# Chunk 0 of a Mamba-style block: its x-projection moved into its convolution, copies a block later, late weight halves on GpSimd

## Reference

```python
x = x + 0.5 * ffn(layernorm(x))      # gate and up 512 -> 1408, silu(g) * u, down -> 512
x = x + mamba(layernorm(x))
x = x + 0.5 * ffn(layernorm(x))
```

```python
proj = einsum('blh,oh->bol', x, W_in); h, gate = split(proj, 2)    # 1024 channels each
h = silu(causal_conv4(h) + conv_b)
ts, B, C = split(einsum('bil,oi->blo', h, Wx), [128, 144])         # the x-projection: 128 + 16 + 16
ts, B, C = rms(ts), rms(B), rms(C)
delta = softplus(Wdt.T @ ts + dt_bias)
s_t = exp(delta_t * A) * s_(t-1) + delta_t * B_t * h_t             # 16 states a channel
y = (sum_n s_t * C_t + D * h) * silu(gate)
return y @ Wout.T
```

## Time and profile before

| | us |
|---|---|
| median of 3 runs | 2893.6 (2881.7 to 2895.21) |
| the profiled execution | 2891.33 |
| its span, first to last instruction | 2889.4 |
| DVE busy in it | 2494.8 |
| PE busy in it | 2412.0 |
| POOL busy in it | 2261.2 |
| first scan starts at | 203.0 |

### The profile page before, as it was taken

One profiled execution on the slowest core, in us unless ns is written; L12 is line 12 of the kernel. 1 busy time (PEld: TensorE's weight loads), 2 busy tenths in 40 slices (PEclk: granted clock), 3 DMA queues, 4 the chain that ended last, 5 costly groups with the idle time before them and its releaser, 6 DMA issues. The chain is left out here.

```text
span 2889.4 us, 38162 instructions
## 1 busy us (share of the span) xinstructions
PE 2412.0 (83%) x12266; PEld 1949.8 (67%) x12266; DVE 2494.8 (86%) x3131; ACT 1757.7 (61%) x2995; POOL 2261.2 (78%) x1371
## 2 busy tenths in 40 slices
PE   6668879788787998889988899889988896599968
PEld 5556667567566776677766777667766775377757
DVE  5559999799888999899989989798988988999973
ACT  5456568667466666576657666667656667465532
POOL 2237859988977989689996889779896899889852
PEclk9789889899888999899998999889999997599979
DMA  7644563674686367955777376964678478355544
GB/s 266 224 149 161 183 228 114 227 258 128 226 286 238 120 203 254 326 163 185 233 262 275 124 221 224 315 211 148 222 256 287 132 263 300 111 192 189 189 163 142
DMA packets 293951, 606.65 MB, mean 210 GB/s; under 512 B 23024, under 2 KB 23792, under 8 KB 293744
## 3 DMA queue, kind: packets, MB, share of 16 engines
q1 hardware_dynamic: 293744, 604.13, 62.4%
HBM read 451.47 MB, written 152.57 MB: 209 GB/s over the span
## 5 line engine op out<-in xcount | busy, mean ns | idle before, releaser
L1893 POOL TENSOR_TENSOR sbuf<-dus,bring 128x1024 f32<-128x1024 f32 x512 | 1222.0, 2403 | 236.2 <-PE pt L1369 128.5
L1520 ACT ACTIVATE pa<-dls,cst 128x512 f32<-128x512 f32 x1024 | 691.4, 688 | 424.2 <-DVE sbuf L1694 416.7
L1369 PE MATMUL pt<-ident,sbuf 128*128 128x128 f32 x4096 | 662.8, 299 | 227.1 <-DVE sbuf L1694 100.6
L1369 PEld LDWEIGHTS pt<-ident,sbuf 128*128 128x128 f32 x4096 | 517.1, 153 | 392.9 <-DVE sbuf L1694 142.3
L1288 PE MATMUL pm<-xT,wring 128*128 128x512 f32 x2816 | 707.8, 400 | 12.7 <-ACT pm L1420 5.5
L1694 DVE TENSOR_TENSOR_SCAN sbuf<-pa,sbuf 128x512 f32<-128x512 f32 x512 | 607.7, 1209 | 61.6 <-ACT pa L1520 52.9
L1694 DVE TENSOR_TENSOR_SCAN sbuf<-pa,carry,sbuf 128x512 f32<-128x512 f32 x512 | 634.5, 1266 | 26.4 <-ACT pa L1520 18.7
L1705 DVE SCALAR_TENSOR_TENSOR acc<-pt,cT,acc 128x512 f32<-128x512 f32 x768 | 547.5, 737 | 76.2 <-PE pt L1369 72.4
L1300 PE MATMUL pm<-wring,act 128*128 128x512 f32 x2176 | 577.8, 408 | 30.4 <-DVE hd L1622 10.3
L1288 PEld LDWEIGHTS pm<-xT,wring 128*128 128x128 f32 x2816 | 518.5, 190 | 115.8 <-issue 15.3
L1311 PE MATMUL pm<-xT,wring 128*128 128x512 f32 x1536 | 430.5, 432 | 79.5 <-DVE hd L1644 27.4
(11 more groups left out here) (130 smaller groups left out, 2266.6 us busy)
## 6 DMA issues: line engine op xcount, KB each, us to landing
wring<-wsp SPq DMA_DIRECT2D x408, 512.0 KB, 4.5
bring<-b_d SPq DMA_DIRECT2D x256, 256.0 KB, 3.9
xn_d<-tb SPq DMA_DIRECT2D x24, 1024.0 KB, 9.8
xnb<-xn_d SPq DMA_DIRECT2D x19, 1024.0 KB, 7.9
x_d<-tb SPq DMA_DIRECT2D x16, 1024.0 KB, 6.2
u_d<-hd SPq DMA_DIRECT2D x64, 256.0 KB, 4.9
sg_d<-hd SPq DMA_DIRECT2D x64, 256.0 KB, 4.4
tb<-x_d SPq DMA_DIRECT2D x16, 1024.0 KB, 7.1
```

What stands on the lines that cost most here:

```text
L1369: ins = e.matmul(pt[u.pt[tt]][:, k * P:(k + 1) * P], sbuf[:, u.s3, k, tt * P:(tt + 1) * P], ident[:, :], is_transpose=True, start=True, st ...
L1520: e.activation(pa[k % 2][:, :], dls[:, k, :], ACT.Exp, scale=col(C_A + (4 * u.ig + k) * N + u.n)).then_inc(S.a_exp, 1)
L1893: e.tensor_tensor(sbuf[:, u.s3, h * m:(h + 1) * m, :], dus[:, h * m:(h + 1) * m, :], bring[:, u.s2:u.s2 + 1, :].broadcast_to([P, m, TC]), ...
```

## The change

Four things change. First, in chunk 0 the steps of the x-projection are listed inside the convolution: step 0 behind block 6's projection, step 1 behind block 7's, steps 2 to 6 behind the last block. They add to the two banks of `pt`, blocks 4 and 5 are made in the two banks of `pa` (six banks for the projection), and there is a fourth tap row. Second, ACT's copy and POOL's subtraction of block i are listed behind the end of block i + 1, in every chunk (`conv_lift`). Third, the last step and `x_out` of chunk 0 are a stage `x_end`, and three of the eight gates stand between it and `dt0`. Fourth, the low halves of the 16 late pieces are made by POOL and no longer by DVE.

```diff
+AHEAD0 = 6
+GATES0 = 3
-OPENING = (("ffn1", 0), ("prep_in", 0), ("dt0", 0), ("gates", 0), ("dt2", 0), ("dt3", 0), ("ffn1", 1),
+OPENING = (("ffn1", 0), ("prep_in", 0), ("x_end", 0), ("gates_a", 0), ("dt0", 0), ("gates_b", 0), ("dt2", 0), ("dt3", 0), ("ffn1", 1),
...
-        u.lo = self.up(self.S.v_piece)
+        u.lo = self.up(self.S.g_piece if late else self.S.v_piece)
...
-        keys = ("aa", 0), ("aa", 1), ("th", 0)
+        keys = ("aa", 0), ("aa", 1), ("th", 0), ("th", 1)
+        x_banks = [(NM + 2, (self.flag,)), (NM + 3, ())]
...
-            u.h, u.key = i % (2 if c else 3), i % 3
+            u.h, u.key = i % (2 if c else 3), i % (3 if c else 4)
...
-            u.bank, u.bank_before = self.bank()
+            if c == 0 and i in (NM, NM + 1):
+                u.bank, u.bank_before = i, ()
+            else:
+                u.bank, u.bank_before = self.bank()
...
+            elif not c and i >= AHEAD0:
+                self.x_step(c, i - AHEAD0, x_banks)
             self.nested(i)
         while opened:
             self.conv_end(opened.pop(0), keys)
+        if self.lifts:
+            self.conv_lift(self.lifts.pop())
...
+        if c == 0:
+            for k in range(NI - AHEAD0, NI - 1):
+                self.x_step(c, k, x_banks)
+            for k in range(2):
+                self.sfree["pa", k] = self.bank_free[NM + k]
+            self.to_close = c, x_banks
+            return
...
         self.free[keys[v.key]] = self.bank_free[v.bank] = (v.u,)
-        v.hi = self.up(S.a_chi)
-        v.lo = self.up(S.g_clo)
+        if self.lifts:
+            self.conv_lift(self.lifts.pop())
+        self.lifts.append(v)
+
+    def conv_lift(self, v):
+
+        S = self.S
+        w = self.add("c", self.step_of(v, "conv_lift"))
+        w.hi = self.up(S.a_chi)
+        w.lo = self.up(S.g_clo)
...
+        if c == 0:
+            for h in range(2):
+                self.sfree["pt", h] = (u.sq[h],)
...
+        elif kind == "x_end":
+            self.close_x()
+        elif kind == "gates_a":
+            self.gates(c, range(GATES0))
+        elif kind == "gates_b":
+            self.gates(c, range(GATES0, NI))
...
+        pm += pa + pt
...
+                    elif u.kind == "whole" and u.late:
+                        q.wait_ge(u.hi)
+                        e.tensor_tensor(staged_out(u)[:, 1, :], staged_in(u), staged_out(u)[:, 0, :],
+                                        ALU.subtract).then_inc(S.g_piece, 1)
```

More of the change, by code:

```diff
@@ L267, in __init__ @@
         self.part_free = [()] * 4
-        self.bank_no, self.bank_free, self.held = 0, [()] * NM, set()
+        self.bank_no, self.bank_free, self.held = 0, [()] * 8, set()
         self.free, self.sfree = {}, {}
@@ L272, in __init__ @@
         self.early = {}
+        self.lifts = []
         self.following = None
@@ L645, in prep_in @@
             self.x_step(c, k, banks)
-        if c:
-            self.next_xT("prep_in")
+        self.next_xT("prep_in")
         self.to_close = c, banks
@@ L663, in conv_end @@
         self.u_out.append(v.kept)
-        self.free["hd", v.h] = (v.hi, v.lo, v.kept)
-        self.x_ready[v.i] = v.hi, v.lo
+        self.free["hd", v.h] = (w.hi, w.lo, v.kept)
+        self.x_ready[v.i] = w.hi, w.lo
     def gate(self, c, i, xT):
@@ L683, in gate, with gates @@
         self.g_out.append(u.kept)
-    def gates(self, c):
+    def gates(self, c, these):
         self.g_out = self.post_ready[c][1]
-        for i in range(NI):
+        for i in these:
             self.gate(c, i, self.xT_of[c])
@@ L1054, in main @@
                 plan.extend((WIN + i, "whole" if light else "both") for i in range(NI))
-            elif kind == "gates":
+            elif kind == "gates_a":
                 plan.extend((WIN + NI + i, "late") for i in range(NI))
@@ L1096, in stage @@
             self.dt0(c)
-        elif kind == "gates":
-            self.gates(c)
+        elif kind == "x_end":
+            self.close_x()
+        elif kind == "gates_a":
+            self.gates(c, range(GATES0))
+        elif kind == "gates_b":
+            self.gates(c, range(GATES0, NI))
         elif kind == "post":
@@ L1195, in macaron @@
         S.v_scan, S.v_cmac = sem("v_scan"), sem("v_cmac")
+        S.g_piece = sem("g_piece")
         S.g_const, S.g_one, S.g_ve, S.g_rs, S.g_nb = sem("g_const"), sem("g_one"), sem("g_ve"), sem("g_rs"), sem("g_nb")
@@ L1229, in macaron @@
         dram_rows = dict(x=x_in, x2=x2_d, x3=x3_d, out=out)
-        conv_row = aa[:, 0, :], aa[:, 1, :], th[:, 0, :]
+        conv_row = aa[:, 0, :], aa[:, 1, :], th[:, 0, :], th[:, 1, :]
         soft_row = {(name, k): b[:, k] for name, b in (("spX", spx), ("spE", spe), ("spW", spw)) for k in range(2)}
@@ L1459, in program @@
                         yield
-                        q.wait_ge(u.u, *u.act_before)
-                        e.activation(act[:, 0, u.i, :], hd[:, u.h, :], ACT.Copy).then_inc(S.a_chi, 1)
+                    elif u.kind == "conv_lift":
+                        v = u.of
+                        q.wait_ge(v.u, *v.act_before)
+                        e.activation(act[:, 0, v.i, :], hd[:, v.h, :], ACT.Copy).then_inc(S.a_chi, 1)
                         yield
@@ L1730, in program @@
                         yield
-                    elif u.kind in ("whole", "part"):
+                    elif u.kind in ("whole", "part") and not u.late:
                         q.wait_ge(u.hi)
@@ L1806, in program @@
                         yield
-                    elif u.kind == "conv_end":
+                    elif u.kind == "conv_lift":
+                        v = u.of
                         q.wait_ge(u.hi)
-                        e.tensor_tensor(act[:, 1, u.i, :], hd[:, u.h, :], act[:, 0, u.i, :],
+                        e.tensor_tensor(act[:, 1, v.i, :], hd[:, v.h, :], act[:, 0, v.i, :],
                                         ALU.subtract).then_inc(S.g_clo, 1)
@@ L1923, in program @@
                         e.memset(lored[:, 2:3], 1.0).then_inc(S.g_one, 1)
+                        yield
+                    elif u.kind == "whole" and u.late:
+                        q.wait_ge(u.hi)
+                        e.tensor_tensor(staged_out(u)[:, 1, :], staged_in(u), staged_out(u)[:, 0, :],
+                                        ALU.subtract).then_inc(S.g_piece, 1)
                         yield
```

## The result

The changed kernel takes 2842.8 us (median of 4 runs, 2835.6 to 2847.9) where the kernel before takes 2889.2 (4 runs, 2881.7 to 2895.2). The ratio is 0.9835, with an interval of 0.9804 to 0.9867: it is faster, by 46 us, and not by the 22 forecast. The time lies outside the range of 2853 to 2896.

A forecast was written before the change was run, and what follows sets the result against it. No engine bounds the whole run; the chain of waits up to the first scan does. Terms 8.0 + 4.0 - 2.2 + 6.1 + 3 + 3 = 21.9 us off 2891.3, plus 2.3 for the median, give 2872 us, range 2853 to 2896.

The forecast's parts named there:

- the rest of the run as a smaller correction: Whole run: the first scan comes 15.9 us earlier and both streams follow; behind it only 3 and 3 us more.
- The later copy: Chunks after the first: copies wait behind the next block's tanh, rows of `hd` still free 9 us early; costed at nothing.
- `Wout` on POOL: Eight late pieces between 700 and 900 us, 17.58 us on DVE, moved to POOL; 3 us gained, bounds 7.5 gained, 3 lost.
- The convolution: Chunk 0, up to the last convolution end: DVE no longer waits for taps; 8.0 us gained, bounds 0 to 13.6.
- the stores of `hd`: Chunk 0's convolution: a row is wanted back after some 10 us, its store takes up to 8.7; 2 us deducted.
- The x-projection: Chunk 0, behind the last convolution end: only one step is left there, 4.1 us in place of 8.1; 4.0 us gained.
- The three gates: Between `x_out` and `dt0`: 9.9 us of PE work fills a 7.7 us hole; 2.2 us lost, bounds 0.6 to 5.5.
- products in idle time: Ahead of `dt0`: the three gates' products on DVE lie in its idle time; no cost counted.
- The late halves at the first scan: Ahead of the first scan: three late subtractions leave DVE, so the scan no longer waits for them; 6.1 us gained.
- the second rival: Shared SBUF port: late subtractions on POOL hold back DVE's softplus or POOL's products; 9.5 us gain remains, 2884; chance 0.08.
- stay in the opening: First rival: the earlier start is partly lost in later waits or full DMA engines; 9 us remain, 2884; chance 0.20.
- The third rival: Chunks 1 to 7: DVE's convolution ends wait for POOL to free rows of `hd`; slower, 2925 us; chance 0.10.

The follow-up runs named there:

- changed, at 0.27: The changed kernel with the list scheduler's margin at 0.27 us instead of 0.30 behind 300 us of its clock; 2868.0 us.
- before, at 0.27: The kernel before with the list scheduler's margin at 0.27 us instead of 0.30 behind 300 us of its clock; 2909.8 us.
- before + later copy, at 0.33: The kernel before plus only the later copy, with the list scheduler's margin at 0.33 us instead of 0.30 behind 300 us of its clock; 2868.4 us.

## Why the prediction was right in direction and wrong in size

**The wrong yardstick.** The prediction took the first scan as the point from which everything follows, and "the rest of the run as a smaller correction". The runs contradict it: the first scan is at 189 to 193 us in six kernels (changed, late halves on DVE, the two of one half on POOL, and the two with fewer gates) whose times go from 2840 to 2882. What does set the time behind it is a balance of two streams that share DVE. One is the scans of a chunk. The other is the projections and convolutions of later chunks, with the delta products that the second half of a chunk's scan needs. I measured the cushion between them: the start of that second half's first scan less the start of POOL's last delta product for it. The product must be stored and loaded again before POOL can use it, about when that first scan starts or up to some 4 us later. Where POOL stood waiting for it, this trip took 13.1, 13.3 and 13.9 us in chunks 3 to 5 and 24.1 in chunk 6 (the kernel without the later copy), from the start of the product to its use. A cushion well below that is a stall. Cushions in us, and DVE idle behind the first scan, from the traces:

| kernel | us | chunk 3 | 4 | 5 | 6 | DVE idle |
|---|---|---|---|---|---|---|
| before | 2891.6 | 21 | 10 | 18 | 25 | 300 |
| before + later copy | 2899.3 | 96 | 98 | 96 | 107 | 325 |
| before + late halves on POOL | 2919.9 | -7 | 10 | 18 | 25 | 342 |
| x-projection, banks and gates only | 2873.5 | 50 | 30 | 22 | 25 | 299 |
| changed, late halves on DVE | 2881.7 | 103 | 100 | 103 | 107 | 309 |
| changed, only the gates' on POOL | 2876.6 | 102 | 101 | 105 | 106 | 296 |
| changed, only Wout's on POOL | 2839.9 | 31 | 31 | 31 | 25 | 282 |
| changed | 2842.8 | 31 | 32 | 31 | 24 | 275 |
| changed, without the later copy | 2951.5 | -10 | 0 | -3 | -1 | 377 |
| changed, at 0.27 | 2868.0 | 45 | 23 | 6 | 25 | 304 |
| before, at 0.27 | 2909.8 | 29 | 25 | -3 | -2 | 310 |
| before + later copy, at 0.33 | 2868.4 | 64 | 66 | 49 | 76 | 280 |

The last three rows are other orders of the same work: the order moves the cushion too, and where it leaves the kernel before -3 and -2 us, POOL waits 8.1 and 19.2 us for the product. But a large cushion by itself is no gain (325 and 309 us idle at some 100 us), and the later copy alone reaches 280 us idle in one order.

**The later copy** was costed at nothing in the later chunks, and alone it is worth nothing that can be told from the merge's luck: 2899.3 and 2902.2, once 2868.4. But it does something, which another part can use. The convolution's ends of chunk 1, without it (before), with it alone, and in the changed kernel (the line of the end, six of eight blocks, the others have other operands):

```profile
L1644 DVE SCALAR_TENSOR_TENSOR hd<-pm,aa x6: 661/664/681, 354.1 to 423.3; 128x512 f32<-128x512 f32 x6
```
```profile
L1657 DVE SCALAR_TENSOR_TENSOR hd<-pm,aa x6: 664/666/684, 352.8 to 412.7; 128x512 f32<-128x512 f32 x6
```
```profile
L1680 DVE SCALAR_TENSOR_TENSOR hd<-pm,aa x6: 666/679/691, 330.0 to 381.5; 128x512 f32<-128x512 f32 x6
```

They go from 69 us to 60 and 51. From first to last end, the convolutions of chunks 1 to 7 take 72 us in the mean before and 63 with the later copy alone, and the cushion grows from 10 to 25 us to some 100. In the kernel before POOL waited for such a product 5.8 us at most (chunk 4), so there was little to gain.

**`Wout` on POOL** was +3 us, and this is the step that was most wrong. It is worth 37 us (2876.6 to 2839.9) in a kernel with the later copy and the scheduler's own margin, all late halves together 7 us at 0.27; over the orders, the four kernels with it there (2839.9, 2842.8, 2860.9, 2868.0) are 25 us below the three without (2874.7, 2876.6, 2881.7) in the mean, and none of the four reaches the three. The prediction gave the 17.6 us of DVE in the earlier trace rows a fraction, DVE being "not the only limit"; the mean says that they count in full, and what is above them is within the scatter of the orders. The move also has a price on the other side: with these pieces on POOL the projection stream falls behind the scans, by about 70 us of cushion (102 to 31 in chunk 3). With the later copy that cushion is there. Without it the scans run dry. This is the kernel without the later copy, what DVE and what POOL waited for in its chunk 6 (total, times, longest), 2228 to 2580 us:

```profile
DVE sbuf L1728 <- POOL sbuf L1928: 22.5, 3, 21.5
```
```profile
POOL sbuf L1928 <- DMA dus<-du_d: 22.8, 2, 19.2
```

and the timelines of POOL, SP's queue and DVE there:

```profile
2406.31 2.41 POOL L1865 TENSOR_TENSOR spw<-spx,spw 128x1024 f32<-128x1024 f32 x1
...
2430.41 7.08 POOL L1928 TENSOR_TENSOR sbuf<-dus,bring 128x1024 f32<-128x1024 f32 x3 [19.19 <-DMA dus<-du_d]
```
```profile
2408.75 0.36 SPq L2113 DMA_DIRECT2D du_d<-spw  x1
2418.41 2.88 SPq L2129 DMA_DIRECT2D dus<-du_d  x2
```
```profile
2432.88 2.34 DVE L1728 TENSOR_TENSOR_SCAN sbuf<-pa,sbuf 128x512 f32<-128x512 f32 x2 [21.54 <-POOL sbuf L1928]
```

The delta product at 2406.3 is stored at 2408.8, loaded at 2418.4, and POOL can use it at 2430.4: 24.1 us for the trip, and the scan stands 21.5 of them. In chunks 3 to 5 the load is issued sooner and POOL waits some 8 us each time; this is chunk 3:

```profile
1382.67 2.40 POOL L1865 TENSOR_TENSOR spw<-spx,spw 128x1024 f32<-128x1024 f32 x1 [0.65 <-DMA spw<-u_d]
...
1395.72 4.73 POOL L1928 TENSOR_TENSOR sbuf<-dus,bring 128x1024 f32<-128x1024 f32 x2 [8.06 <-DMA dus<-du_d]
```

In the changed kernel the trip of chunk 6 ends with a wait of 1.5 us:

```profile
2285.24 2.42 POOL L1867 TENSOR_TENSOR spw<-spx,spw 128x1024 f32<-128x1024 f32 x1
...
2310.31 9.41 POOL L1930 TENSOR_TENSOR sbuf<-dus,bring 128x1024 f32<-128x1024 f32 x4 [1.54 <-DMA dus<-du_d]
```

So the changed kernel runs at the brink in chunk 6, where its cushion of 24 us is nearly what the trip needs; in chunks 3 to 5 it has 31 us where some 14 would do. Windows of DVE over chunks 3, 4 and 6, without the later copy and in the changed kernel:

```profile
1185.00:1545.00 360.00, 304.75 (x381) 0.92 0.65 223
1545.00:1919.00 374.00, 316.23 (x411) 0.91 0.67 228
2228.00:2580.00 352.00, 283.69 (x347) 0.83 0.62 210
```
```profile
1189.00:1505.00 316.00, 299.19 (x373) 0.95 0.69 229
1505.00:1828.00 323.00, 297.38 (x377) 0.95 0.69 234
2142.00:2455.00 313.00, 273.49 (x328) 0.84 0.64 217
```

Idle time is 55, 58 and 68 us against 17, 26 and 40: 99 us more, most of the 109 between the two kernels. The busy time differs by 35 us here because the chunks' borders hold other work; over the whole stretch behind the first scan it grows by 5.5 us only. POOL's waits for that one product are 8.1, 8.0, 7.9 and 19.2 us in chunks 3 to 6, together 43; what the rest of the idle time waits for is spread over PE and ACT, and that it follows from the same lag is argued, not shown.

**The opening's terms.** The convolution gave 8.0 us as forecast, in part by luck: the stores of `hd`, costed at 2 us, took 6.2 (0.65 and 5.56), and this was made good by the waits for the tanh (2.4 us), which went too, and by a start 0.9 us earlier (DVE's instruction in front of the first taps at 113.4 before, at 112.5 now). The x-projection gave 5.0 us and not 4.0: the granted clock was 1.00 from 149.3 to 151.0 us, that is in the last step, where the prediction had taken 0.50, and `x_out` stands at 150.3 (forecast 151.3). The three gates took 8.4 us and not 9.9, and put `dt0` at 159 (forecast 161), 12.1 us earlier than before. DVE's part of it is only 8.1 us earlier, for what the prediction called "products in idle time" on DVE held `dt0` up: the third product waits 4.94 us for a store of its row. The late halves at the first scan, +6.1, gave nothing (191.4 with them on DVE, 192.7 on POOL). The prediction counted this twice: with three gates in front, two of the three subtractions leave that place by themselves (one of 2.82 us is left with them on DVE). And on POOL a subtraction fell among its products, the second rival's mechanism, at 2.25 us and not 1.29. The rule of the Trainium skill ("SBUF — State Buffer", section "SBUF: two separate sides") that such instructions exclude each other agrees with this row too: DVE's L1700 (2.77 us, two inputs in SBUF) ran until 186.8. Only there did POOL pay. The sum is 10.3 in place of 15.9 us. That the x-projection, its banks and the gates are worth 18 us (2891.6 to 2873.5) with a first scan only 1.2 us earlier would fit with their working through the projection stream, as chunk 3's cushion goes from 21 to 50, but DVE's idle time hardly falls (300 to 299) in that profile, the kernel's longest run.

**The rivals.** The gain did not stay in the opening; more of it came behind. The port did what the second rival said at one place, and its price there was at most 3.5 us (192.7 against 189.2 with the gates' pieces on DVE), with POOL's second product in front as well and the first scan's own scatter in it. The third rival did not come: in chunks 1 to 7 no convolution end in the changed kernel waits for POOL for its row; the slack of the earlier trace rows held. That the parts might only pay together was not among the rivals, and it is what happened: all late halves on POOL cost 78 us without the later copy in the new kernel (2873.5 to 2951.5; 28 in the kernel before, 2891.6 to 2919.9, which is within the merge's luck), and gain 39 with it.

**What stays open.** Why the projection stream falls behind by just so much when POOL makes `Wout`'s pieces was not tried alone: POOL makes them until 813.5 and DVE until 766.2 us, and the scans get ahead by DVE's time, but how the 70 us of cushion divide between the two isn't shown. Nor is it shown why DVE's idle time falls in the changed kernel's own order: the later copy alone, with no piece moved, came from 325 to 280 us idle and from 2899.3 to 2868.4 us by another order. Whether an order that spends the cushion would give the same without the move to POOL was not tried, nor were the parts of the 18 us one by one. And no kernel here beats the changed one by more than can be told: 2839.9 and 2842.8 are alike.

## What to carry to other kernels

When two streams of work share a busy engine, look for how far one is ahead of the other at the point where it hands over, and compare that with the length of the handover (here a store and a load, 13 to 24 us): a part that enlarges the cushion can be worth nothing until another part spends it, and two parts must then be priced together. Time taken off an engine that is 86% busy counted in full here in the mean of the orders (DVE some 15 us less busy, the time 25 us shorter, between 7 and 39 from one pair to another), as long as that cushion held. And where an order is made by a list scheduler, run the same work in two or three other orders before a difference of one per cent is put down to an edit.

## What the runs showed of the hardware

Not expected was how long DVE pays for a subtraction with both inputs in SBUF beside a busy POOL. The same instruction took 0.66 us and, in the middle of eight, 2.18 us, with three in a row at 8.37 us in front of the first scan, as the earlier trace rows had it before (8.41 for three). The traces show what it waits for. With `Wout`'s halves on POOL, the subtraction of 2.82 us in front of the first scan ends at 189.25, 0.54 us behind this product of POOL (188.71):

```profile
185.56 3.15 POOL L1931 TENSOR_TENSOR sbuf<-dus,bring 128x1024 f32<-128x1024 f32 x1
188.67 2.82 POOL L1868 TENSOR_TENSOR dus<-dls,dus 128x1024 f32<-128x1024 f32 x1
```

POOL's next product then took 2.82 us where it took 2.36 in the changed kernel. In the kernel before, each of the three subtractions of the earlier trace rows ended 0.55 us behind a product of POOL in the same way, and the longest (7.54 us) stood beside three products in a row. POOL's took 1.28 us in the middle of its sixteen and 2.25 at most:

```profile
L1964 POOL TENSOR_TENSOR wring<-tb,wring x16: 1261/1280/2249, 139.4 to 809.9; 128x512 fp32r<-128x512 f32 x16
```

So an instruction that is twice as slow on POOL was the cheaper of the two for the kernel. The other thing not expected was the store of a 256 KB row of `hd`: a DVE instruction stood up to 5.6 us for it in the opening, with the DMA engines full there.
